# Second attention: scores as two single-pass products over high and low halves, operands sent ahead through a ring

## What is computed

```python
xn = layer_norm(x)
q, k, v = xn @ wq + bq, xn @ wk + bk, xn @ wv + bv            # 12 heads of 48
logits = einsum('nthd,nThd->nhtT', q, k) / sqrt(48)           # 256 x 256 per head
logits += einsum(q, rel_pos_0[coords])[..., :, None] + einsum(q, rel_pos_1[coords])[..., None, :]
out = einsum('nhtT,nThd->nthd', softmax(logits), v) @ wo + bo
```

## Time and profile before

| | |
|---|---|
| median of 3 runs | 840.53 us (839.22 to 841.15) |
| the profiled execution's own time | 842.7 us |
| its span on the core | 840.9 us |
| granted TensorE clock, mean share of full | 0.955 |
| busy: PE / DVE / ACT / POOL | 761.4 / 518.4 / 434.7 / 128.8 us |
| attention 1, from its first q and k products to the last output | 411.4 to 772.5 us |

### The profile page before, as it was taken

One profiled execution on the slowest core, in us unless ns is written; L12 is line 12 of the kernel. 1 busy time (PEld: TensorE's weight loads), 2 busy tenths in 40 slices (PEclk: granted clock), 3 DMA queues, 4 the chain that ended last, 5 costly groups with the idle time before them and its releaser, 6 DMA issues.

```text
span 840.9 us, 18486 instructions
## 1 busy us (share of the span) xinstructions
PE 761.4 (91%) x6570; PEld 614.5 (73%) x6570; DVE 518.4 (62%) x1548; ACT 434.7 (52%) x1421; POOL 128.8 (15%) x231
## 2 busy tenths in 40 slices
PE   5898989889898977799969999999999999997998
PEld 4675756667575744699958787878787878675998
DVE  5457686776677676475326757575757576474551
ACT  2246565554646555554336656565646465454442
POOL 9101010111011010242220101010101010100221
PEclk9589999999999998799979999999999999799999
DMA  5615402011010100100040304030303030400001
GB/s 98 155 28 125 79 9 37 13 25 20 18 23 15 32 7 1 39 1 2 2 76 9 69 10 67 12 66 12 66 16 64 14 64 8 68 2 1 21 20 38
DMA packets 39163, 30.06 MB, mean 36 GB/s; under 512 B 12678, under 2 KB 37026, under 8 KB 39072
## 3 DMA queue, kind: packets, MB, share of 16 engines
q1 hardware_dynamic: 36130, 26.61, 16.7%
q0 software_dynamic: 2048, 1.89, 1.2%
q10 hardware_dynamic: 894, 0.37, 0.4%
HBM read 8.77 MB, written 1.57 MB: 12 GB/s over the span
## 4 chain that ended last, share of the span: by engine, by line
PE 78%; DVE 11%; issue 4%; ACT 3%; DMA 2%; SPq 1%; POOL 1%; ACTq 0%; DVEq 0%; POOLq 0%
PE bank L1300 11%; PE bank L1386 8%; PE bank L540 7%; PE bank L520 7%; PE bank L1327 5%; PE bank L1307 5%; PE bank L1170 5%; PE bank L1001 4%; PE bank L977 4%; PE bank L1346 4%; PE bank L1102 3%; DVE Pb L722 3%; PE bank L1442 3%; PE bank L1028 2%; DVE nmax L701 2%
## 5 line engine op out<-in xcount | busy, mean ns | idle before, releaser
L711 ACT ACTIVATE Pb<-bank,nmax 128x256 f32<-128x256 f32 (+1 forms) x432 | 192.0, 452 | 83.0 <-DVE nmax L701 80.4
L701 DVE TENSOR_REDUCE nmax<-bank 128x2 f32<-128x392 f32 (+2 forms) x240 | 138.9, 579 | 53.3 <-PE bank L1300 37.2
L722 DVE TENSOR_SCALAR Pb<-Pb,rsum 128x196 f32<-128x196 f32 (+2 forms) x432 | 136.6, 354 | 8.5
L741 ACT COPY area<-bank 98x392 f32<-98x392 f32 (+1 forms) x144 | 77.4, 539 | 91.5 <-PE bank L1307 75.1
L1300 PE MATMUL bank<-QK 80*128 80x256 f32 x384 | 109.1, 410 | 10.7 <-DMA QK<-rel_dense 8.5
L1300 PEld LDWEIGHTS bank<-QK 80*128 80x128 f32 x384 | 70.0, 200 | 32.1 <-issue 17.4
L711 ACT ACTIVATION_READ_ACCUMULATOR Pb<-bank,nmax 128x1 f32 x432 | 87.4, 202 | 0.0
L1001 PE MATMUL bank<-ident,Pb 128*98 128x128 f32 x384 | 63.7, 291 | 20.2 <-DVE Pb L722 20.2
L529 ACT ACTIVATE area<-bank,fc1b 128x256 f32<-128x256 f32 x96 | 45.1, 475 | 54.1 <-PE bank L520 46.1
L741 DVE COPY area<-bank 60x128 f32<-60x128 f32 (+2 forms) x96 | 43.3, 451 | 38.5 <-PE bank L1004 20.5
L1001 PEld LDWEIGHTS bank<-ident,Pb 128*98 128x98 f32 x384 | 41.6, 133 | 34.0 <-DVE Pb L722 28.9
(11 more groups left out here) (150 smaller groups left out, 1479.9 us busy)
## 6 DMA issues: line engine op xcount, KB each, us to landing
QK<-dense SPq DMA_DIRECT2D x32, 288.0 KB, 6.2
QK<-dense SPq DMA_DIRECT2D x48, 64.0 KB, 2.4
QK<-dense SPq DMA_DIRECT2D x92, 28.0 KB
QK<-rel_dense SPq DMA_DIRECT2D x32, 48.0 KB, 3.1
QK<-rel_dense POOLq DMA_DIRECT2D x32, 48.0 KB, 2.9
out<-x_all SPq DMA_DIRECT2D x8, 192.0 KB, 2.0
x_all<-in_x SPq DMA_DIRECT2D x1, 1152.0 KB, 7.6
QK<-in_c_hot SPq DMA_DIRECT2D x2, 384.0 KB, 4.7
```

Of the source, the lines that this page charges most:

```text
L701: nc.vector.tensor_reduce(nmax[0:sc.shape[0], u % 3, 0:sc.shape[1]], sc, AX.X, ALU.max, negate=True).then_inc(self.m_rdy, 1)
L711: nc.scalar.activation(Pb[u % 3][0:rows, t, 0:cols], sc[:, t, :], ACT.Exp, bias=nmax[0:rows, u % 3, t:t + 1], accum_out=esum[0:rows, u % 3 ...
L722: nc.vector.tensor_scalar(Pb[u % 3][0:rows, t, 0:keep], Pb[u % 3][0:rows, t, 0:keep], rsum[0:rows, u % 3, t:t + 1], None, ALU.mult).then_i ...
L741: copy(*self.pt_views(u)).then_inc(self.pt[self.pt_engine(u)], 1)
```

## The change

The scores of a unit become four float32r matmuls over 128 rows. Their key operand (`ring[:, 2]`) has 48 rows of high parts of k, 48 rows of low parts, and the 32 one-hot rows. The query operand exists twice: `ring[:, 0]` has the high parts of q twice and the high parts of the relative terms, `ring[:, 1]` the low parts in the same places. Both are multiplied with the same keys and summed in PSUM.

High and low parts are made before the transfers. ACT casts three groups of q and then of k at once (`act_high`, in slots 2 and 4). POOL subtracts to get the low parts, three groups at a time. ACT casts all four relative pieces, DVE subtracts to get their low parts from PSUM. SP issues nothing any more in this stage: all transfers are POOL's, 12 for each half image (2 of the high k, 2 of the low k, 4 of q with both parts in one, 4 relative), and the second half's subtractions stand behind the first half's transfers in POOL's order. A piece is now three tiles of 256 numbers in a row at both ends.

The targets are a ring of three half images in place of two whole ones. Scores wait for half an image at units 0 and 6. All fronts stand one slot earlier; the statistics of the next but one image are taken in slot 10. The one-hot rows are loaded by POOL, after all of its work in MLP 0, into the ring's 18 key tiles; PE's wait for them stays where it was.

```diff
-K1REL = D1
-K1ROWS = K1REL + 2 * H
+K1REL = 2 * D1
+RING = 3 * 6
...
+        parts = lent("parts", [CH, 3 * NPAIR, T], F32R)
...
+        operands = lent("operands", [P, 3 * RING, T])
+        QK = [operands[:, 2 * HEADS * i:2 * HEADS * (i + 1), :] for i in range(2)]
+        ring = sb("ring", [P, 3, RING, T], F32R)
+        Q1, K1 = [ring[:, i] for i in range(2)], ring[:, 2]
...
-        rows1 = [(K1[i][K1REL:K1ROWS], per_head(a["c_hot1"])) for i in range(2)]
+        rows1 = (ring[K1REL:P, 2], per_head(a["c_hot1"], RING))
...
+                if u == self.STATS_SLOT and 2 * n.pair + n.par + 2 < B:
+                    self.dve_stats(eng, n.next().next())
...
+            XT_SLOT = 1
+            STATS_SLOT = 10
             G_USES = (10, 10)
             G_OUTS = (11, 11)
-            V_SLOT = 7
+            V_SLOT = 6
             VALUES_BEHIND = 1
...
             def emit_scores(self, eng, n, u):
-                p = n.parity
-                if u == 0:
-                    eng.wait_ge(self.scat, n.at(64, 64))
-                    eng.wait_ge(self.relscat, n.at(64, 64))
-                    eng.wait_ge(self.relscat_w, n.at(64, 64))
+                half, at = u // 6, self.first_tile(n, u // 6) + 3 * (u % 2) + u // 2 % 3
+                if u % 6 == 0:
+                    eng.wait_ge(self.scat[half], n.at(16 * 8, 16 * 8))
+                    eng.wait_ge(self.relscat[half], n.at(16 * 4, 16 * 4))
                 for t in range(NT):
-                    mm = nc.tensor.matmul(S_BANK[u % 3][:, t * T:(t + 1) * T], Q1[p][:, u, t * P:(t + 1) * P],
-                                          K1[p][:, u, :], start=True, stop=True)
+                    for i in range(2):
+                        mm = nc.tensor.matmul(S_BANK[u % 3][:, t * T:(t + 1) * T], Q1[i][:, at, t * P:(t + 1) * P],
+                                              K1[:, at, :], start=(i == 0), stop=(i == 1))
                 return mm
+            def first_tile(self, n, half):
+                return 6 * ((2 * number(n) + half) % 3)
...
             def act_q(self, eng, n, g):
                 eng.wait_ge(self.g_rdy[0], n.at(10, 2 + g))
-                if g == 0:
-                    if n.counts(64, 0):
-                        eng.wait_ge(self.scat, n.at(64, 0))
-                    if n.counts(10, 0):
-                        eng.wait_ge(self.g_rdy[1], n.at(10, 0))
+                if g == 0 and n.counts(10, 0):
+                    eng.wait_ge(self.g_rdy[1], n.at(10, 0))
+                if g % 3 == 0 and n.counts(2, g // 3 - 1):
+                    eng.wait_ge(self.q_low, n.at(2, g // 3 - 1))
                 nc.scalar.activation(self.qd[:, g, :], G_BANK[0][0:CH, 0:T], ACT.Identity,
                                      bias=qb1[:, g:g + 1]).then_inc(self.g_out[0], 1)
...
+            def act_high(self, eng, n, half):
+                if n.counts(16 * 8, 0):
+                    eng.wait_ge(self.scat[half], n.at(16 * 8, 0))
+                if n.counts(2, half - 1):
+                    eng.wait_ge(self.k_low, n.at(2, half - 1))
+                for b, (dst, src, done) in enumerate(((self.qh, self.qd, self.q_high), (self.kh, self.kd, self.k_high))):
+                    eng.wait_ge(self.g_out[b], n.at(11, 4 + 3 * half))
+                    nc.scalar.copy(dst[:, 3 * half:3 * half + 3, :], src[:, 3 * half:3 * half + 3, :]).then_inc(done, 1)
...
-                if g == 0:
-                    if n.counts(64, 0):
-                        eng.wait_ge(self.scat, n.at(64, 0))
+                if g % 3 == 0 and n.counts(16 * 8, 0):
+                    eng.wait_ge(self.scat[g // 3], n.at(16 * 8, 0))
...
             def act_rel(self, eng, n):
+                for b in range(2):
+                    eng.wait_ge(self.g_rdy[b], n.at(10, 8))
+                    for s in range(2):
+                        nc.scalar.copy(*self.rel_views(b, s, 0)).then_inc(self.rel_high[b], 1)
...
             def dve_rel(self, eng, n):
+                for b in range(2):
+                    eng.wait_ge(self.g_rdy[b], n.at(10, 8))
+                    for s in range(2):
+                        eng.wait_ge(self.rel_high[b], n.at(2, s + 1))
+                        low, bank_rows = self.rel_views(b, s, 1)
+                        high_rows, _ = self.rel_views(b, s, 0)
+                        nc.vector.tensor_tensor(low, bank_rows, high_rows.bitcast(F32), ALU.subtract)\
+                          .then_inc(self.g_out[b], 1)
...
+            def pool_front(self, eng, n):
+                for half in range(2):
+                    used = (-self.NU, 6 - self.NU)[half]
+                    groups, at = slice(3 * half, 3 * half + 3), self.first_tile(n, half)
+                    def send(rows, o, j, src):
+                        eng.dma_start(ring[rows, o, at + 3 * j:at + 3 * j + 3, :], src).then_inc(self.scat[half], 16)
+                    eng.wait_ge(self.k_high, n.at(2, half + 1))
+                    nc.gpsimd.tensor_tensor(self.kl[:, groups, :], self.kd[:, groups, :],
+                                            self.kh[:, groups, :].bitcast(F32), ALU.subtract).then_inc(self.k_low, 1)
+                    eng.wait_ge(self.q_high, n.at(2, half + 1))
+                    if n.counts(16 * 8, 0):
+                        eng.wait_ge(self.scat[half], n.at(16 * 8, 0))
+                    nc.gpsimd.tensor_tensor(self.ql[:, groups, :], self.qd[:, groups, :],
+                                            self.qh[:, groups, :].bitcast(F32), ALU.subtract).then_inc(self.q_low, 1)
+                    if n.counts(self.NU, used):
+                        eng.wait_ge(self.s_rdy, n.at(self.NU, used))
+                    land(eng, "pool")
                     for j in range(2):
+                        send(slice(0, D1), 2, j, self.kh[D1 * j:D1 * (j + 1), groups, :])
+                    eng.wait_ge(self.k_low, n.at(2, half + 1))
+                    land(eng, "pool")
                     for j in range(2):
+                        send(slice(D1, 2 * D1), 2, j, self.kl[D1 * j:D1 * (j + 1), groups, :])
+                    eng.wait_ge(self.q_low, n.at(2, half + 1))
+                    land(eng, "pool")
+                    for j in range(2):
+                        for row in (0, D1):
+                            send(slice(row, row + D1), slice(0, 2), j, self.qhl[D1 * j:D1 * (j + 1), :, groups, :])
                     for b in range(2):
                         eng.wait_ge(self.g_out[b], n.at(11, 9))
+                    land(eng, "pool")
+                    for table in range(2):
+                        for j in range(2):
+                            row, src = K1REL + H * table, 64 * table + 32 * half + H * j
+                            eng.dma_start(ring[row:row + H, 0:2, at + 3 * j:at + 3 * j + 3, :],
+                                          rel_parts[src:src + H]).then_inc(self.relscat[half], 16)
...
+                self.pe_fronts = {1: [self.pe_transpose_x], 2: each(self.pe_qk, (0, 1, 2)), 3: each(self.pe_qk, (3, 4)),
+                                  4: each(self.pe_qk, (5,)) + [self.pe_rel], 6: each(self.pe_v, (0,)),
+                                  7: each(self.pe_v, (1,))}
+                self.act_fronts = {1: [self.act_xn], 2: each(self.act_q, (0, 1, 2)) + each(self.act_high, (0,)),
+                                   3: each(self.act_q, (3, 4)),
+                                   4: each(self.act_q, (5,)) + each(self.act_high, (1,)), 5: [self.act_rel], 6: each(self.act_v, (0,)),
+                                   7: each(self.act_v, (1,))}
+                self.dve_fronts = {0: [self.dve_xhat], 1: [self.dve_xn], 2: each(self.dve_k, (0, 1, 2)),
+                                   3: each(self.dve_k, (3, 4)), 4: each(self.dve_k, (5,)), 5: [self.dve_rel],
+                                   6: each(self.dve_v, (0,)), 7: each(self.dve_v, (1,))}
+            def run_pool(self, eng, following, after_front):
+                self.norm.pool_rstd(eng, Img(0, 1))
+                self.pool_front(eng, Img(0, 0))
+                after_front(eng)
+                def step(n, has_prev, has_next):
+                    if has_next:
+                        self.pool_front(eng, n.next())
+                    else:
+                        following(eng)
+                    self.pool_xbias(eng, n)
+                    if 2 * n.pair + n.par + 2 < B:
+                        self.norm.pool_rstd(eng, n.next().next())
+                image_loop(eng, step)
...
-            stage_start(sp, 1)
-            for dst, src in rows1:
-                sp.dma_start(dst, src).then_inc(ld_rows1, 16)
-            a1.sp(sp)
...
             m0.run_pool(pool, pool_weights1, lambda e: a1.norm.pool_rstd(e, Img(0, 0)))
+            pool.dma_start(*rows1).then_inc(ld_rows1, 16)
             stage_start(pool, 2)
...
-            pe.wait_ge(ld_rows1, 16 * len(rows1))
+            pe.wait_ge(ld_rows1, 16)
```

(19 more changed lines are left out.)

93 lines of the change are left out of this document (29 added, 64 removed).

## The result

The changed kernel takes 865.6 us (median of 4 runs, 856.5 to 868.1), the kernel before 840.8 beside it: 1.026 times as long (1.021 to 1.031). The forecast was 834 us, in a range of 806 to 864. The profiled execution took 868.1 us with a span of 866.3, against 842.7 and 840.9.

| stretch of the profiled execution | before | after | change | forecast |
|---|---|---|---|---|
| to the first product of MLP 0 (code not changed) | 344.7 | 347.6 | +2.9 | 0 |
| from there to the first projection of attention 1 | 137.4 | 144.7 | +7.3 | +6.2 |
| first to last projection, seven periods | 285.7 | 297.3 | +11.6 | -12.9 |
| from there to the end | 73.1 | 76.7 | +3.6 | 0 |

A forecast was written before the change was run, and what follows sets the result against it. PE was taken to bound attention 1, busy 41.2 of 41.9 us an image. From 842.7: scores -38.4, `xbias` -6, seven images' waits +27.3, last image +2.4, start +8 give 836.0, as a median 834 us; range 806 to 864.

The forecast's parts named there:

- Scores, 0.40 us a unit: PE's scores in attention 1: four matmuls take 0.47 us instead of 0.87, saving 38.4 us over 96 units.
- What is taken from PE's scores counts in full: PE's chain in attention 1: savings count in full until an engine with less room or a transfer is late.
- 0.7 us an image for DVE's lack of room: Slots without front work: PE 3.0 us against DVE about 2.9 for two, so waits of 0.7 us an image (0 to 2).
- POOL's subtractions, 2.0 us an image: Slots 8 and 9: second half's subtractions block DVE, or the first half arrives late; 2.0 us an image for both together.
- The clock I had tied to a wait of the transfers alone: Slower rival, chance 0.20: first half late in slot 9, half clock behind waits from about 1.7 us; 872 us, or 851.
- The `xbias` stalls, -6: Around slot 7: `xbias` moves to the next image's slot 1, so six stalls of 1.0 us go.
- ACT's casts, 0.8 us: Slot 2: casts end 1.6 us after group 2's q and delay group 3's copy, 0.8 us an image (0 to 1.5).
- Start, +8: Start of attention 1: late one-hot rows idle PE 5.6 us, half clock follows; parts land 8 us later (2 to 14).
- Arrival: Slot 9: first half just in time or 2 to 3 us late; POOL's issues 15.4 us an image, relative pieces landing in 2.9.
- The last image, -4.8 + 2.4: Last image: DVE and ACT hold the chain half of the time, so half of its 4.8 us is given back.
- The rival "pays nothing": Waits of slots 2 to 9 come to 5 us or more an image, clock at full: 842 to 848 us; chance 0.09.

The follow-up runs named there:

- run 6: Kernel before, with only the fronts of attention 1 one slot forward (statistics and POOL's order with them), scores and transfers as before: 835.1 us, 0.992 of before.
- run 7: Kernel of run 6, each score made as two products over 16-bit views of the same q and k, no low parts made or moved: 813.7 us, 0.969.
- run 5: Changed kernel, the second half's POOL subtractions put ahead of the wait for the first half's position rows and their four transfers: 846.3 us, 1.004 of before.
- run 12: Kernel of run 11, with ACT's casts made group by group behind each q instead of behind the third: 832.4 us, 0.990 of before.
- run 9: Changed kernel, DVE makes the normalized x of slot 1 ahead of the sum behind the back projection: 860.7 us.
- run 10: Changed kernel, POOL issues the one-hot rows at the end of attention 0, ahead of its MLP 0 work: 860.7 us.
- run 11: Changed kernel with the three orders of run 5, run 9 and run 10 together: 838.2 us, 0.997 of before.
- run 13: Kernel of run 12, with the position rows' eight transfers of an image issued by SP instead of POOL: 888.3 us, 1.057 of before.

## Why the prediction was wrong

It said faster, and the stretch between first and last projection missed by 24.5 us.

- **Scores, 0.40 us a unit.** Right on PE (0.48 us), wrong on the path. "What is taken from PE's scores counts in full" is the first step that failed: by runs 6 and 7 21.4 of 38.4 us count. I gave 0.7 us an image for DVE's lack of room; what was lost is 2.7 (4.8 saved, 2.1 seen). The place was wrong too. The forecast looked for it in the slots without fronts, PE 3.0 us against DVE 2.9 for two of them. There run 7 keeps all of the saving, and loses it at three waits: the normalized x, the next image's first scores, the transposes of x.
- **POOL's subtractions, 2.0 us an image** for DVE or the arrival, each hiding the other. The mechanism was right and the size was not: 4.08 us of stall and half clock behind it, and run 5 gives back 3.6 us in the short periods, with 0.9 us of arrival still in what is left. Two things were mis-sized. The pair is held once, by both subtractions without a pause, where I had two separate blocks of up to 1.8, half covered. And it was put into slots 8 and 9, beside the late rows; it came in slot 7, ahead of them, so neither hid the other. The clock I had tied to a wait of the transfers alone; the same length of wait behind DVE did it.
- **The `xbias` stalls, -6.** Run 6 gives -6, but not by the forecast's working, and partly by luck. The 1.0 us that I read off is ACT's time in the chain. PE's own wait there was 0.24 to 0.77 us, in four images of six and 2.2 us in all; a pause with half clock that run 6's trace lacks makes up much of the rest.
- **ACT's casts, 0.8 us.** Right: 0.9 an image, 5.8 us in run 12.
- **Left out: the normalized x.** The move into slot 1 put it behind DVE's wait for the projection. 5 us by run 9.
- **Start, +8.** About right in sum: the stretch came out at +7.3 against +6.2. The working was not: POOL's issue price a piece did not apply (0.75 us for 576 pieces, not 5.7), and PE paused 3.3 us, not 5.6, with no half clock behind it. From the end of MLP 0 to the first score it is 5.5 us more, not 8. The first half's position rows took 7.9 us to land in place of the 2.9 that I took, in part with PE idle and the clock falling.
- **Arrival.** POOL's issuing, about 13 of 22 us busy in an image, did not bound, and in the changed kernel the arrival did so once. It came out where the stall was gone (run 5), at 8.3 us in six images, 3.5 of them in one.
- **The last image, -4.8 + 2.4, and MLP 1, 0.** Measured +0.9 in the period and +3.6 behind it: a fall of the clock in each, and 2.0 us of POOL's closing DRAIN. No step had either.

The rival "pays nothing" came nearest in time, and by another sum than its own. Runs 5 and 9 to 12 come to 832 us, the forecast's figure, for a kernel that was not the one predicted.

## What to carry to other kernels

Before work is taken from the engine that bounds, list place by place what it will then wait for. Here units with nothing due gave the whole saving, and three hand-overs an image took back about half of it. An average of busy shares, or a sum over two slots, showed none of them. Elementwise work put on POOL is priced by what DVE has to do in the same microseconds and by what POOL does on both sides of it, so place it beside PE's long fronts; here the same instructions in another order were worth 19 us. When an order on one queue is loosened, look at what it had been holding back.

## What the runs showed of the hardware

- A pair of DVE normalizations, 0.62 us alone, lasted 4.59 beside two POOL subtractions of 96x768 without a pause, 5.40 with two issues between them, 2.83 with 0.56 us of idleness between them. Issues alone did not hold it (0.62). In each of these holds the normalization ended 0.16 us after POOL's operation.
- The Trainium skill (SBUF — State Buffer, Who interferes with whom) has whoever issues first keep the shared pair for its whole instruction. The trace agrees that the other is held to the end of POOL's instruction; but DVE's had started first, by 0.5 us in the kernel before and by 0.3 to 0.55 in most images of the changed one, and alone it takes 0.35. And for two POOL operations in a row the hold reached over both, which that rule doesn't give.
- A transfer issued by POOL cost 0.50 to 0.57 us of POOL at 96, 144 and 288 KB alike.
- POOL's closing DRAIN took 3.9 us where it had issued 34 transfers and 8.0 where it had issued 195; with eight of an image's transfers moved to SP (run 13, 131 by POOL) it took 11.6. In the last two cases the span ended with it.
- A pause of PE of 3.3 us at 414.3 was followed by full clock (ten products in 1.38 us at 417.6), where 4 us at a quarter of PE's time were followed by half clock in each image.
